# Casts of the count matrix to f16: narrower first range, later ScalarE cast, one cast moved to GpSimd

## The chip, the cores and the metric

The kernel runs on one core of a Trainium2 chip. The metric is the device time of the program in microseconds, the median of several executions. Engines are named as in the profile: PE is TensorE, DVE is VectorE, ACT is ScalarE, POOL is GpSimd, SP is SyncE.

## The reference: what is computed

A graph network of four layers over N = 1024 nodes with D = 512 features and 16384 edges. The graph arrives as two index lists, and three of the layers need it as a matrix. The part that the change touches stands in the first layer:

```
adj = zeros((N, N)); adj[row, col] = 1; adj[col, row] = 1; adj = adj + eye(N)
adj = adj / max(adj.sum(axis=1), 1)
cur = x @ W + b
for i in range(3): cur = adj @ cur; out = out + dw[i + 1] * cur
x = layernorm(x + relu(out))
```

The later layers sum over the edges (with their counts), take means over them, and compute an attention with a softmax over them; each ends in a residual sum and a layernorm.

## The kernel before

**The count matrix.** The edges are worked off in 64 groups of 256 (`NG`). For each, PE multiplies one-hot matrices that DVE and ACT build, and DVE adds the product to a window of the f32 count matrix `c32` (128 partitions x 8 tiles of rows x 1024 columns); this is `add_window`, line 1274, and each addition raises the semaphore `win_free`. The same loop on PE also computes h = xW in f32 (line 774). When the 64th window is added, `c32` is complete. On PE, `attention_columns` (line 810, 32 f32 matmuls of 40 columns for the last layer) stands between the last group and what follows.

**The passage.** From `c32` to the 0/1 matrix `adj` the kernel goes in four steps, tile by tile:

- Casts: `c32` goes to the f16 matrix `cst`, in column ranges given by `CAST_COLS = ((0, 256), (256, 512), (512, 1024))`. For the first two ranges ACT casts row tiles 0 to 2 (`CA` = 3) and DVE row tiles 3 to 7. Of the third range ACT casts tile 7 at once and tiles 5 and 6 later, DVE casts tiles 0 and 1 (line 1343) and later tiles 2 to 4 (line 1360).
- Transposes: `ct_block(t)` on PE (line 871) transposes the t-th block of 128 columns of all 8 row tiles of `cst` into one of three banks of PSUM. It waits for the casts of its range: `chunk_of(t)` is the index of the range in which column block t lies. Block t from 3 on also waits for a free bank.
- Evictions: ACT copies the bank to `cts[:, t, :]` (line 437), and raises `cts_ready`.
- DVE builds row tile t of `adj` from `cst[:, t, :]` and `cts[:, t, :]` (line 1354, a scalar_tensor_tensor with a row sum, 1358 adds the diagonal), and raises `adj_ready`. This needs all 1024 columns of row tile t of `cst`.

PE then multiplies: for each j it waits for `adj_ready` j + 1 and issues 8 matmuls of 512 columns (line 886) that use row tile j of `adj`, with `ct_block(j + 3)` between. After the eighth come the second half of the first step (line 897) and the second and third steps (lines 907, 925).

**The order.** It is written by hand. Each engine has one queue in program order; between engines there are semaphores. On PE stand ct_block(0), (1), then waits for the last pieces of h, (2), (3), then the matmuls. On DVE stand the two casts of line 1313, `h_lower(7)` (line 1279, the low half of the last tile of h), the cast of line 1343, and the loop over t with line 1360 behind t = 1. On ACT stand the three casts, three evictions, the cast of tiles 5 and 6, and five evictions. POOL has done its part of the constants by then: its last instruction ahead of the passage scales a bias (`b0w` times `wsum`, line 394, once DVE has summed the weights), the next (line 383) waits for the first weight's high half, which ACT makes behind the passage. A branch for edges outside their window (`flag(.., 0)`) is not taken.

Of the kernel before, what the change touches and what calls it, by code (L numbers as in the profile page):

```python
# [48 lines left out]
H_FROM = 4  # L49
H_TO = 31  # L50
ZERO_ACT = 6
CAST_COLS = ((0, 256), (256, 512), (512, 1024))
CT_BANKS = (0, 1, 5)
WINDOW_BANKS = (0, 1, 6, 7)

# [40 lines left out]
def build(nc, x, xT, src, dst, W0, b0, dw, W1T, b1, wc, wn, b2, W3, W3T, b3, b3T, aw, ab, out):  # L96
    with ExitStack() as ctx:
# [248 lines left out]
        def _(pool):  # L346
# [31 lines left out]
            pool.affine_select(out=sel[:], in_=sel[:], compare_op=ALU.not_equal, fill=1.0, base=0,  # L378
                               pattern=[[-1, H + 1], [0, P]], channel_multiplier=1).then_inc(S["const_ready"], 1)

            def split_lo(n, name, raw):
                pool.wait_ge(S["w_hi"], n)
                pool.tensor_tensor(ws[:, SLOT[name], 1], raw, ws[:, SLOT[name], 0], ALU.subtract).then_inc(S["w_lo"], 1)  # L383
# [7 lines left out]
            pool.wait_ge(S["wba_a"], 1)  # L391
            pool.tensor_tensor(wba[:], wba[:], wbc[:].unsqueeze(2).broadcast_to([P, KT, H]), ALU.mult).then_inc(S["wba_in"], 1)
            pool.wait_ge(S["wsum_in"], 1)
            pool.tensor_scalar(b0w, b0w, wsum[:], None, ALU.mult).then_inc(S["bias_in"], 1)
            split_lo(1, "W1", stage[:, 0])
            split_lo(2, "wc", stage[:, 1])
# [38 lines left out]
        def _(act):  # L435
# [65 lines left out]
            for c0, c1 in CAST_COLS[0:2]:  # L501
                copy(cst[:, 0:CA, c0:c1], c32[:, 0:CA, c0:c1]).then_inc(S["cst_act"], 1)
            c0, c1 = CAST_COLS[2]
            copy(cst[:, 7:NT, c0:c1], c32[:, 7:NT, c0:c1]).then_inc(S["cst_act"], 1)
            for t in range(NT):
                act.wait_ge(S["ct_done"], t + 1)
                copy(cts[:, t, :], bank16(CT_BANKS[t % 3])).then_inc(S["cts_ready"], 1)
                if t == 2:
                    copy(cst[:, 5:7, c0:c1], c32[:, 5:7, c0:c1]).then_inc(S["cst_act"], 1)
            act.wait_ge(S["const_ready"], 12)  # L510


# [216 lines left out]
        def _(pe):  # L729
# [133 lines left out]
            pe.wait_ge(S["win_free"], NG)  # L863

            def ct_block(t):
                pe.wait_ge(S["cst_act"], (1, 2, 4)[chunk_of(t)])
                pe.wait_ge(S["cst_dve"], (1, 2, 4)[chunk_of(t)])
                if t >= 3:
                    pe.wait_ge(S["cts_ready"], t - 2)
                for j in range(NT):  # L870
                    ins = pe.transpose(bank16(CT_BANKS[t % 3])[:, j * P:(j + 1) * P], cst[:, j, t * P:(t + 1) * P], id16[:])
                ins.then_inc(S["ct_done"], 1)
# [320 lines left out]
        def _(dve):  # L1193
# [123 lines left out]
            with dve.If(flag(dve, 0)):  # L1317

                dve.wait_ge(S["cst_dve"], 2)
                dve.wait_ge(S["cst_act"], 3)  # L1320
                for a in range(NT):
                    ts(iota_n[:, a * P:(a + 1) * P], iota_lo[:], float(a * P), None, ALU.add).then_inc(S["far_iota"], 1)
                dve.wait_ge(S["far_iota"], NT)
                cols_s = nslo[:].rearrange("p g c -> p (g c)")
                cols_f = far.rearrange("p g c -> p (g c)")
                CHUNKS = NC * NG
                with dve.Fori(0, NT) as a:
                    with dve.Fori(0, CHUNKS) as e:
                        n = a * CHUNKS + e
                        dve.wait_ge(S["far_free"], n + 1)  # L1330
                        ts(oh_far, iota_n, cols_f[:, bass.ds(e, 1)], None, ALU.is_equal).then_inc(S["far_hot"], 1)
                        ts(oh_lo, iota_lo[:], cols_s[:, bass.ds(e, 1)], 0.0, ALU.add, ALU.is_equal).then_inc(S["far_hot"], 1)
                    dve.wait_ge(S["far_done"], a + 1)

                    ts(far, far, -float(N), None, ALU.add).then_inc(S["far_added"], 1)
                    tt(c32[:, a, :], c32[:, a, :], ps[:, 0:2, :].rearrange("p a n -> p (a n)"), ALU.add).then_inc(S["far_added"], 1)
                    dve.wait_ge(S["far_added"], a * 2 + 2)
                for j in range(NT):
                    dve.tensor_copy(cst[:, j, :], c32[:, j, :]).then_inc(S["far_cast"], 1)
                dve.wait_ge(S["far_cast"], NT)  # L1340
            dve.wait_ge(S["const_ready"], 12)
            c0, c1 = CAST_COLS[2]
            dve.tensor_copy(cst[:, 0:2, c0:c1], c32[:, 0:2, c0:c1]).then_inc(S["cst_dve"], 1)

            for t in range(NT):
                dve.wait_ge(S["cts_ready"], t + 1)
                if t == 0:
                    dve.wait_ge(S["cst_dve"], 3)
                    dve.wait_ge(S["cst_act"], 2)
                elif t == 2:  # L1350
                    dve.wait_ge(S["cst_dve"], 4)
                elif t == 5:
                    dve.wait_ge(S["cst_act"], 4)
                stt(adj[:, t, :], cst[:, t, :], -1.0, cts[:, t, :], ALU.mult, ALU.is_lt,
                    accum_out=deg[:, t:t + 1]).then_inc(S["adj_sum"], 1)
                dve.wait_ge(S["adj_sum"], t + 1)
                diag = adj[:, t, t * P:(t + 1) * P]
                tt(diag, diag, id16[:], ALU.add).then_inc(S["adj_ready"], 1)
                if t == 1:
                    dve.tensor_copy(cst[:, 2:5, c0:c1], c32[:, 2:5, c0:c1]).then_inc(S["cst_dve"], 1)  # L1360
# [438 lines left out]
```

## Time and profile before

| | us |
|---|---|
| median of 3 runs | 411.85 (411.67 to 411.90) |
| the profiled execution, its own time | 411.46 |
| its span, first to last instruction | 409.5 |
| PE busy | 379.4 (93%) |
| DVE busy | 278.0 (68%) |
| ACT busy | 244.3 (60%) |
| POOL busy | 92.8 (23%) |

Times in the rows are microseconds from the start of the span. A row of the timeline has the start, the duration, the engine, the line, the operation, out<-in with shapes and the count of instructions merged in it; in brackets stands how long the engine was idle before it, and who ended that. Consecutive instructions of DVE or ACT overlap by about 0.09 us in these records. The chain of waits is followed back from the last instruction. PEclk is the granted clock of TensorE, 1.00 for 2.4 GHz and 0.50 for 1.2 GHz.

### The profile page before, as it was taken

The page shows a single profiled execution, that of the slowest core. Times are in us where ns is not written, and L with a number is a line of the kernel's source. Part 1 is how long each engine was busy: PE and PEld are TensorE (multiplying, and loading weights), DVE is VectorE, ACT ScalarE, POOL GpSimd, SP SyncE. Part 2 cuts the span into 40 slices and gives each one's busy share as a digit, 9 for nine tenths or more (in the row PEclk, how much of TensorE's full clock was granted, in tenths as well). Part 3 has the DMA queues.
Part 4 walks back from the last instruction along what each step waited for, and adds up shares of the span by engine and source line. Part 5 has one row for each costly group of instructions (what it writes and reads, how often), then busy time and mean ns, then how long its engine had stood idle before and what let it go on. Part 6 is the DMA issues. An engine that isn't in the chain of part 4 may idle for free.

```text
span 409.5 us, 8229 instructions
## 1 busy us (share of the span) xinstructions
PE 379.4 (93%) x2844; PEld 225.4 (55%) x2844; DVE 278.0 (68%) x603; ACT 244.3 (60%) x406; POOL 92.8 (23%) x85
## 2 busy tenths in 40 slices
PE   1799889999999998999999999999899999999980
PEld 1344438544444443444445454445457889999980
DVE  7768998838995775206633222554699688999974
ACT  9779785475822246202665221247774999999434
POOL 4510000029920167200764000133100000112110
PEclk9999998999999999999999999999999999999996
DMA  5940005006000000000000000000001112210005
GB/s 192 390 151 2 1 0 205 4 0 206 1 0 2 0 0 3 2 0 2 0 0 2 0 0 3 0 0 2 1 2 49 58 64 93 104 55 2 4 3 206
DMA packets 10040, 18.54 MB, mean 45 GB/s; under 512 B 2128, under 2 KB 2320, under 8 KB 10000
## 3 DMA queue, kind: packets, MB, share of 16 engines
q1 hardware_dynamic: 9136, 14.86, 10.4%
q10 hardware_dynamic: 864, 3.15, 2.2%
q8 instruction: 25, 0.41, 0.4%
q14 instruction: 15, 0.12, 0.1%
HBM read 15.87 MB, written 2.13 MB: 44 GB/s over the span
## 4 chain that ended last, share of the span: by engine, by line
PE 72%; DVE 16%; issue 5%; ACT 3%; DVEq 2%; POOL 1%; ACTq 0%; POOLq 0%
PE ps L741 15%; PE ps L1120 9%; PE ps L968 7%; PE ps L1013 7%; PE ps L925 7%; PE ps L907 7%; PE ps L1061 7%; PE ps L774 4%; PE ps L897 3%; DVE c L1274 3%; PE ps L886 3%; PE ps L795 2%; DVE big L1510 1%; DVE adj L1255 1%; DVE cts L1560 1%
## 5 line engine op out<-in xcount | busy, mean ns | idle before, releaser
L741 PE MATMUL ps<-big,xTs 128*128 128x512 f16 x384 | 85.5, 380 | 1.4 <-ACT xTs L437 1.4
L741 PEld LDWEIGHTS ps<-big,xTs 128*128 128x128 f16 (+1 forms) x384 | 36.8, 98 | 44.0 <-issue 2.1
L648 ACT ACTIVATE big<-big,uvt 128x1024 bf16<-128x1024 f32 x55 | 59.0, 1149 | 0.0
L409 POOL TENSOR_TENSOR big<-xcur,big x24 | 27.7, 1155 | 125.2 <-ACT xcur L530 124.8
L529 ACT ACTIVATE big<-xcur,nmr,rstd (+1 forms) x24 | 19.5, 813 | 36.8 <-DVE nmr L1380 36.8
L774 PE MATMUL ps<-big,xTs 128*128 128x512 f32 x64 | 35.7, 655 | 0.0
L437 ACT ACTIVATE xTs<-ps 128x512 f16<-128x512 f32 (+2 forms) x24 | 20.1, 878 | 21.7 <-PE ps L968 19.0
L437 ACT ACTIVATE big<-ps 128x512 f16<-128x512 f32 (+2 forms) x17 | 9.7, 572 | 34.5 <-PE ps L741 24.6
L1274 DVE TENSOR_TENSOR c<-c,ps 128x80 f32 (+31 forms) x64 | 23.3, 364 | 9.7 <-PE ps L795 6.6
L1061 PE MATMUL ps<-big,cst 128*128 128x260 f16 x256 | 29.8, 275 | 0.0
L383 POOL TENSOR_TENSOR big<-xTs,big 128x2048 f16<-128x2048 f32 x4 | 16.2, 4076 | 59.9 <-ACT big L437 59.9
L968 PE MATMUL ps<-cst,big 128*128 128x512 f16 x128 | 27.8, 380 | 1.6 <-DVE xcur L1451 1.6
L795 PE MATMUL ps<-adj,cts 128*128 128x80 f16 (+31 forms) x128 | 21.0, 271 | 8.7 <-DVE c L1274 4.6
L420 POOL TENSOR_TENSOR xcur<-xcur,c 128x512 f32<-128x512 f32 x6 | 7.1, 1185 | 95.5 <-DVE c L1594 95.5
L795 PEld LDWEIGHTS ps<-adj,cts 128*128 128x128 f16 x128 | 11.4, 109 | 31.4 <-issue 16.6
L1013 PE MATMUL ps<-big,cts 128*128 128x512 f16 x128 | 28.0, 379 | 0.0
L925 PE MATMUL ps<-big,adj 128*128 128x512 f16 x128 | 27.9, 380 | 0.0
L907 PE MATMUL ps<-big,adj 128*128 128x512 f16 x128 | 27.8, 380 | 0.0
L1061 PEld LDWEIGHTS ps<-big,cst 128*128 128x128 f16 x256 | 24.3, 96 | 4.8
L460 ACT ACTIVATE cts<-iota_lo,early 128x128 f16<-128x128 f16 x80 | 25.4, 391 | 0.4
L1255 DVE TENSOR_TENSOR adj<-adj,early 128x160 f16<-128x160 f16 (+31 forms) x64 | 22.3, 390 | 0.1
L968 PEld LDWEIGHTS ps<-cst,big 128*128 128x128 f16 x128 | 12.4, 98 | 16.9 <-DVE xcur L1451 2.1
(206 smaller groups left out, 678.3 us busy)
## 6 DMA issues: line engine op xcount, KB each, us to landing
big<-u_rows ACTq DMA_DIRECT2D x6, 512.0 KB, 3.4
xTs<-in_xT SPq DMA_DIRECT2D x2, 1024.0 KB, 9.3
xcur<-in_x SPq DMA_DIRECT2D x1, 2048.0 KB, 17.5
out<-xcur SPq DMA_DIRECT2D x8, 256.0 KB, 2.1
big<-in_W SPq DMA_DIRECT2D x1, 1024.0 KB, 6.0
cts<-in_W3T SPq DMA_DIRECT2D x1, 1024.0 KB, 12.9
xTs<-in_W1T SPq DMA_DIRECT2D x1, 1024.0 KB, 5.4
xTs<-in_wc SPq DMA_DIRECT2D x1, 1024.0 KB, 8.1
```

The source lines that it names most:

```text
L437: return act.activation(o, i, ACT.Copy, scale=scale, **kw)
L648: act.activation(above[:, a % AHEAD, :], uf[:, h % 2], ACT.Relu, scale=BIG, bias=vb[:, j, h:h + 1]).then_inc(S["above_in"], 1)
L741: return mm(bank, lhs(k)[a], rhs(k)[b], start=start and k == 0 and n == 0, stop=stop and k == KT - 1 and n == 2)
L774: ins = mm(bank, xT32[:, k, t * P:(t + 1) * P], w0raw[:, k, :], start=k == 0, stop=k == KT - 1)
L795: ins = mm(ps[:, WINDOW_BANKS[w % 4], 0:n], left, hot_key[:, r, w % 2 * NC * n:(w % 2 + 1) * NC * n].rearrange("p (k c) -> p k c", c=NC)[: ...
L907: ins = mm(ps[:, t, :], adj[:, j, t * P:(t + 1) * P], cur[:, 1, v, j, :], start=n == 0 and v == 0, stop=n == NT - 1 and v == 1)
L925: ins = mm(ps[:, t, :], adj[:, j, bass.ds(t * P, P)], cur[:, 0, v, j, :], start=n == 0 and v == 0, stop=n == NT - 1 and v == 1)
L968: ins = mm(ps[:, half * KT + k, :], cur[:, 1, v, j, k * P:(k + 1) * P], c[:, j, half * HALF:(half + 1) * HALF], start=c is cst and j == 0 ...
L1013: ins = mm(ps[:, t, :], c[:, j, bass.ds(t * P, P)], cur[:, 0, v, j, :], start=c is cts and j == 0 and v == 0, stop=c is parts[-1] and j == ...
L1061: ins = mm(ps[:, DENSE_BANK[i], 0:4 * (DH + 1)], cst[:, j, t * P:(t + 1) * P], yh[:, j, v, 4 * half:4 * half + 4, DH + 1:YW], start=j == 0 ...
L1120: ins = mm(o, cz[h % CZ][:, j, t * P:(t + 1) * P], yh[:, j, v, h, :], start=j == 0 and v == 0, stop=j == NT - 1 and v == 1)
L1274: tt(cells, cells, ps[:, WINDOW_BANKS[w % 4], 0:NT * m].rearrange("p (a w) -> p a w", w=m), ALU.add).then_inc(S["win_free"], 1)
```

## The change

The first range of columns is 128 wide instead of 256, the second 384 instead of 256. ACT no longer casts tile 7 of the third range ahead of its evictions; behind the third eviction it casts tiles 5 to 7 instead of 5 and 6. The cast of tiles 0 and 1 of the third range moves from DVE to POOL, where it stands behind the computation for `wba` and ahead of the scaling of `b0w`; it waits for all 64 windows and raises a new semaphore `cst_pool`. PE waits for `cst_pool` ahead of ct_block(4) to (7), DVE ahead of row tile 0 of `adj`. The other counts of the semaphores follow.

```
-CAST_COLS = ((0, 256), (256, 512), (512, 1024))
+CAST_COLS = ((0, 128), (128, 512), (512, 1024))
 # POOL
             pool.wait_ge(S["wsum_in"], 1)
+            pool.wait_ge(S["win_free"], NG)
+            pool.tensor_copy(cst[:, 0:2, c0:c1], c32[:, 0:2, c0:c1]).then_inc(S["cst_pool"], 1)
             pool.tensor_scalar(b0w, b0w, wsum[:], None, ALU.mult).then_inc(S["bias_in"], 1)
 # ACT
             c0, c1 = CAST_COLS[2]
-            copy(cst[:, 7:NT, c0:c1], c32[:, 7:NT, c0:c1]).then_inc(S["cst_act"], 1)
...
                 if t == 2:
-                    copy(cst[:, 5:7, c0:c1], c32[:, 5:7, c0:c1]).then_inc(S["cst_act"], 1)
+                    copy(cst[:, 5:NT, c0:c1], c32[:, 5:NT, c0:c1]).then_inc(S["cst_act"], 1)
 # PE
-                pe.wait_ge(S["cst_act"], (1, 2, 4)[chunk_of(t)])
-                pe.wait_ge(S["cst_dve"], (1, 2, 4)[chunk_of(t)])
+                pe.wait_ge(S["cst_act"], chunk_of(t) + 1)
+                pe.wait_ge(S["cst_dve"], chunk_of(t) + 1)
+                if chunk_of(t) == 2:
+                    pe.wait_ge(S["cst_pool"], 1)
 # DVE
-            dve.tensor_copy(cst[:, 0:2, c0:c1], c32[:, 0:2, c0:c1]).then_inc(S["cst_dve"], 1)
...
                 if t == 0:
-                    dve.wait_ge(S["cst_dve"], 3)
+                    dve.wait_ge(S["cst_pool"], 1)
+                    dve.wait_ge(S["cst_dve"], 2)
                     dve.wait_ge(S["cst_act"], 2)
                 elif t == 2:
-                    dve.wait_ge(S["cst_dve"], 4)
+                    dve.wait_ge(S["cst_dve"], 3)
                 elif t == 5:
-                    dve.wait_ge(S["cst_act"], 4)
+                    dve.wait_ge(S["cst_act"], 3)
```

DVE's queue from the first cast to the first tile of `adj` (line 1313 casts, 1279 is `h_lower(7)`, 1343 casts tiles 0 and 1, 1354 builds `adj`; `c` is `c32`, the branch not taken is left out), before:

```order
L1313 CAST cst<-c 128x5x256 [waits win_free]
L1313 CAST cst<-c 128x5x256
L1279 TENSOR_TENSOR big<-ps,big 128x512 [waits acc0]
...
L1343 CAST cst<-c 128x2x512 [waits const_ready]
L1354 SCALAR_TENSOR_TENSOR adj,deg<-cst,cts 128x1024 [waits cst_act,cst_dve,cts_ready]
L1358 TENSOR_TENSOR adj<-adj,id 128x128 [waits adj_sum]
```

and now (the lines are shifted by 5 or 6):

```order
L1318 CAST cst<-c 128x5x128 [waits win_free]
L1318 CAST cst<-c 128x5x384
L1284 TENSOR_TENSOR big<-ps,big 128x512 [waits acc0]
...
L1360 SCALAR_TENSOR_TENSOR adj,deg<-cst,cts 128x1024 [waits cst_dve,cst_pool,cst_act,cts_ready,const_ready]
L1364 TENSOR_TENSOR adj<-adj,id 128x128 [waits adj_sum]
```

The third cast has left the queue, and the first tile of `adj` waits for POOL as well. POOL's queue at the same place, before (`wba` and `big` hold small weights and the bias `b0w`):

```order
L390 TENSOR_TENSOR wba<-abT 128x32 [waits small_in]
L392 TENSOR_TENSOR wba<-wba,wbc 128x32 [waits wba_a]
L394 TENSOR_SCALAR big<-big,wsum 128x512 [waits wsum_in]
L383 TENSOR_TENSOR big<-xTs,big 128x2048 [waits w_hi] x2
L387 TENSOR_TENSOR acc<-acc,big 128x512 [waits acc_r,bias_in]
```

and now:

```order
L392 TENSOR_TENSOR wba<-abT 128x32 [waits small_in]
L394 TENSOR_TENSOR wba<-wba,wbc 128x32 [waits wba_a]
L397 CAST cst<-c 128x2x512 [waits win_free,wsum_in]
L398 TENSOR_SCALAR big<-big,wsum 128x512
L385 TENSOR_TENSOR big<-xTs,big 128x2048 [waits w_hi] x2
```

The cast has come in, and the scaling of the bias behind it waits for the windows too. ACT's queue of casts and evictions (`cts<-ps`), before:

```order
L437 ACTIVATE cst<-c 128x3x256 [waits win_free]
L437 ACTIVATE cst<-c 128x3x256
L437 ACTIVATE cst<-c 128x512
L437 ACTIVATE cts<-ps 128x1024 [waits ct_done] x3
L437 ACTIVATE cst<-c 128x2x512
L437 ACTIVATE cts<-ps 128x1024 [waits ct_done] x5
```

and now:

```order
L441 ACTIVATE cst<-c 128x3x128 [waits win_free]
L441 ACTIVATE cst<-c 128x3x384
L441 ACTIVATE cts<-ps 128x1024 [waits ct_done] x3
L441 ACTIVATE cst<-c 128x3x512
L441 ACTIVATE cts<-ps 128x1024 [waits ct_done] x5
```

One cast less stands ahead of the first eviction, and a longer one behind the third.

## Rows read from the trace of the kernel before

**Rows 1.** The page, its part 4: shares of the whole chain by engine.

```profile
PE 72%; DVE 16%; issue 5%; ACT 3%; DVEq 2%; POOL 1%; ACTq 0%; POOLq 0%
```

**Rows 2.** The chain in order of time: start, duration, engine, tile, line.

```profile
64.42 3.50 PE ps L810 x32
...
67.94 1.02 PE ps L871 x8
...
68.99 1.03 ACT cts L437
...
75.73 1.90 PE ps L886 x8
```

**Rows 3.** Timeline of DVE in the passage.

```profile
66.84 1.82 DVE L1313 CAST cst<-c 128x1280 f16<-128x1280 f32 x2
68.58 0.68 DVE L1279 TENSOR_TENSOR big<-ps,big 128x512 f16<-128x512 f32 x1
69.17 0.68 DVE L1343 CAST cst<-c 128x1024 f16<-128x1024 f32 x1
70.05 1.23 DVE L1354 SCALAR_TENSOR_TENSOR adj<-cst,cts 128x1024 f16<-128x1024 f16 x1 [0.20 <-ACT cts L437]
...
71.46 1.22 DVE L1354 SCALAR_TENSOR_TENSOR adj<-cst,cts 128x1024 f16<-128x1024 f16 x1
...
72.86 1.22 DVE L1360 CAST cst<-c 128x1536 f16<-128x1536 f32 x1
```

**Rows 4.** Timeline of ACT: the casts ahead of the evictions, and the late one.

```profile
66.84 2.10 ACT L437 ACTIVATE cst<-c 128x768 f16<-128x768 f32 x3 [1.79 <-DVE c L1274]
...
71.72 1.07 ACT L437 ACTIVATE cst<-c 128x1024 f16<-128x1024 f32 x1
```

**Rows 5.** Timeline of PE, and of its weight loads (PEld).

```profile
67.94 3.57 PE L871 MATMUL ps<-id,cst 128*128 128x128 f16 x32
71.60 3.63 PE L886 MATMUL ps<-big,adj 128*128 128x512 f16 x16
...
75.73 1.41 PEld L886 LDWEIGHTS ps<-big,adj 128*128 128x128 f16 x8 [0.24 <-DVE adj L1358]
```

**Rows 6.** Stretches: length, PE, PEld, DVE, ACT, POOL busy, PEclk, DMA; two matmul rows of PE.

```profile
64.57:67.98 3.41, 3.38 (x31) 3.30 (x31) 3.10 (x6) 1.62 (x3) 0.00 (x0) 1.00 0.72 274
67.98:71.39 3.41, 3.41 (x32) 3.27 (x32) 3.18 (x6) 3.36 (x5) 0.00 (x0) 0.50 0.89 318
...
16.78:20.19 3.41, 3.28 (x12) 1.44 (x11) 2.52 (x11) 1.96 (x6) 0.08 (x1) 1.00 1.05 388
...
20.42 2.02 PE L774 MATMUL ps<-big,xTs 128*128 128x512 f32 x2
...
24.31 0.64 PE L774 MATMUL ps<-big,xTs 128*128 128x512 f32 x1
```

**Rows 7.** Timelines of POOL and DVE where both are at work.

```profile
12.20 0.84 POOL L368 TENSOR_TENSOR cst<-cst 64x256 f32<-64x256 f32 x1
...
12.19 0.27 DVE L1255 TENSOR_TENSOR adj<-adj,early 128x224 f16<-128x224 f16 x1
...
12.37 0.80 DVE L1255 TENSOR_TENSOR adj<-adj,early 128x224 f16<-128x224 f16 x1
...
111.33 4.06 POOL L383 TENSOR_TENSOR big<-xTs,big 128x2048 f16<-128x2048 f32 x1
...
113.16 2.26 DVE L1427 TENSOR_SCALAR cnt<-cnt 128x8 f32<-128x8 f32 x1
```

**Rows 8.** Groups of POOL by line and shape: total, mean ns of one.

```profile
L409 POOL TENSOR_TENSOR big<-xcur,big x24 | 27.7, 1155 | 125.2 <-ACT xcur L530 124.8 <-issue 0.4
...
L383 POOL TENSOR_TENSOR big<-xTs,big 128x2048 f16<-128x2048 f32 x4 | 16.2, 4076 | 59.9 <-ACT big L437 59.9
...
L394 POOL TENSOR_SCALAR big<-big,wsum 128x512 f32<-128x512 f32 x1 | 1.6, 1562 | 0.0
...
L364 POOL CAST cst<-cst 64x256 f32<-64x256 int32 x1 | 0.4, 389 | 0.1
```

More of the change, by code:

```diff
@@ L379, in _ @@
                                pattern=[[-1, H + 1], [0, P]], channel_multiplier=1).then_inc(S["const_ready"], 1)
+            c0, c1 = CAST_COLS[2]
             def split_lo(n, name, raw):
@@ L1319, in _ @@
                 dve.wait_ge(S["cst_dve"], 2)
-                dve.wait_ge(S["cst_act"], 3)
+                dve.wait_ge(S["cst_act"], 2)
+                dve.wait_ge(S["cst_pool"], 1)
                 for a in range(NT):
@@ L1347, in _ @@
                 if t == 0:
-                    dve.wait_ge(S["cst_dve"], 3)
+                    dve.wait_ge(S["cst_pool"], 1)
+                    dve.wait_ge(S["cst_dve"], 2)
                     dve.wait_ge(S["cst_act"], 2)
                 elif t == 2:
-                    dve.wait_ge(S["cst_dve"], 4)
+                    dve.wait_ge(S["cst_dve"], 3)
                 elif t == 5:
-                    dve.wait_ge(S["cst_act"], 4)
+                    dve.wait_ge(S["cst_act"], 3)
                 stt(adj[:, t, :], cst[:, t, :], -1.0, cts[:, t, :], ALU.mult, ALU.is_lt,
```

## The prediction

> **What bounds the kernel now.** The first view is the chain of waits, by engine: PE is 72% of what ended last [rows 1], so a change counts only where it moves PE. The second is the same chain in order of time, around the change [rows 2]. The reader is to see that it never passes through a cast ahead of the first eviction: the f32 products of line 810 hold PE until 67.92, the first eight transposes run from 67.94 to 68.96, ACT evicts from 68.99, DVE starts the first tile of the adjacency at 70.05, and at 75.73 the chain goes back to PE for good. The third view is the timelines of DVE, ACT and PE [rows 3 to 5], which show how close the other engines were. DVE's first two casts take 66.84 to 68.66, so one takes 0.95 and the first is done at 67.79, 0.13 ahead of PE. ACT's three casts end at 68.94, 0.02 ahead of the end of the transposes. DVE is ready at 69.85, 0.20 ahead of the eviction. The weight loads stand idle for 0.24 at 75.73, which cost PE about 0.06; at 71.6 PE waited about 0.1. Those two gaps are all the time that PE loses between 67.94 and the end of this stage.
>
> **The narrower first range.** DVE's casts take 0.68 for 2 tiles of 512 columns, 1.22 for 3, and 0.95 for 5 of 256 [rows 3]. These three fit 0.14 us plus 1.05 ns for each column of the pairs of tiles, an odd tile counting as a pair (1, 2 and 3 pairs). So 5 tiles of 128 take 0.14 + 3 x 128 x 1.05 ns = 0.55, and 5 of 384 take 1.35; together as much as before. The first is done at 67.39 instead of 67.79. ACT's part is ready earlier too. The gain is nil: the transposes wait for PE itself until 67.92. The second block of transposes now hangs on the second cast, which ends at 68.67 if nothing stops it, 0.1 ahead of need (67.94 + 8 x 0.107 = 68.80). This margin is what the change gives away.
>
> **ACT.** Its third cast, 2.10 less two of 0.75, 0.6 us, goes from the front [rows 4]. ACT is then free at 68.4 instead of 68.94, but the first eviction waits for PE until 68.96: gain at most 0.02, taken as nothing. Behind the third eviction it casts 1536 elements a partition instead of 1024: 1.07 + 0.45 = 1.5. The fourth eviction ends near 74.2 instead of 73.7, and DVE wants it at 75.6; PE wants the cast at about 75.0 and has it by 73.3. Both are covered, with 1.4 us to spare.
>
> **DVE.** The cast of line 1343 takes 0.59 of its queue away. It ended 0.20 ahead of the eviction that DVE waits for, so by itself its removal gives nothing; DVE's spare time there becomes 0.8.
>
> **The cast on POOL.** No row shows POOL casting f32 to f16 at this size. The nearest are the cast of 256 elements in 0.39 and the two-input operations, 1.155 for 512 and 4.076 for 2048, that is 0.18 plus 1.90 ns an element [rows 8]. Upper bound: as slow as a two-input one, 2.1. Lower bound: half its rate, for one input, 1.1. The small cast scaled up gives 1.56 with its fixed part counted four times. I take 1.2, nearest to the lower bound, as the small cast less a fixed part of 0.15 comes to 0.94 ns an element. If POOL ran undisturbed from 66.9 it would be done by 68.1, two microseconds ahead of need.
>
> It isn't undisturbed. Two places show DVE and POOL shutting each other out [rows 7]. At 113.16 DVE works on 8 elements and takes 2.26 us: it ends at 115.42, when POOL's operation of 111.33 to 115.39 does. At 12.20 POOL starts an operation while DVE runs the first of two equal ones; DVE's first takes 0.27, its second, which has nothing to wait for, 0.80, and it ends 0.13 after POOL's, at 13.17. So POOL goes in between two operations that stand back to back on DVE, and the second waits until POOL is through. The two casts of DVE are such a pair, and POOL's cast is released by the same semaphore as the first.
>
> The Trainium skill, "SBUF — State Buffer", section "Who interferes with whom", says that DVE in a mode that uses both ports and GpSimd hold one pair of ports by turns, for the whole instruction, and that the order of issue decides who waits. By that rule this change costs something whichever starts first. Both rows above agree with it (0.80 and 2.26 us).
>
> **The sum.** DVE's first cast ends at 67.39; POOL has the port until 68.6; DVE's second cast, 1.3 beyond that, ends at 69.9 instead of 68.66. The second block of transposes starts at 70.0 instead of 68.8. PE at 1.2 GHz needs 0.86 for it, and 0.2 passes until ACT sees the end: eviction 71.05 to 72.05. DVE's second tile then starts at 72.06 instead of 71.46: 0.6 late. The first tile: `h_lower` ends at 70.5, but POOL's queue has a second operation right behind the cast, the scaling of the bias, moved here from 27.84. Its bounds are 1.56 (its row [rows 8]) and 0.7 (half of the cast's 1.2 and a little). It follows DVE's second cast, from 69.9 to 70.6, and DVE's first tile, with two operands in SBUF, starts at 70.6 instead of 70.05: 0.55 late, which the 0.6 of the second tile swallows; by the upper bound it is 1.4 late. From there the chain on DVE is the old one, and the third column's matmuls go from 75.73 to about 76.3. PE itself is no bound there: its remaining transposes end near 72.0 and 16 matmuls at 0.216 and 8 transposes bring it to 75.9. After that PE is continuous as before, so the shift stays. Sum +0.6, with the scaling's length somewhat towards its upper bound +0.7. Against the profiled execution 411.46 + 0.7 = 412.2; it lay 0.39 under the median, and on the median the forecast is 411.85 + 0.7 = **412.6**. The bounds of POOL's two durations make it +0.4 to +1.4.
>
> **Rivals.**
>
> *A, the clock stays down: slower.* From 67.98 to 71.39 PE ran at 1.2 GHz, and it rose to 2.4 behind a stretch in which PE was busy throughout, 3.41 of 3.41 [rows 6]. My sum puts a gap of 1.0 us into it. Early in the span PE was busy for 3.28 of 3.41 from 16.78 to 20.19, and the two f32 matmuls behind took 1.01 each, half rate; at 24.31 one took 0.64 with its fill (the clock column reads 1.00 there only because its record begins later). Against it: what those matmuls fed in was sparser than a string of transposes. If the clock stays down for as long again, to 74.8, the rest of the transposes ends at 72.6, the 16 matmuls (3.45 us at full rate, 1.1 of it done by 74.8) at 77.15, the next transposes at 77.6: 1.9 late. Time 411.85 + 1.9 = 413.8. It decides once PE's gap in that stretch is long enough.
>
> *B, nothing happens.* POOL's cast and scaling, 1.2 and up to 1.56, run from 66.9 to 69.7 beside DVE's casts, which would need the port to be free for both. For it: near 28.6 DVE's operations kept their pace beside the scaling. Then all is in place at 70.05, and the time is 411.85. It can be no gain: the two gaps of PE, 0.15 together, are out of reach, as the first eviction waits for PE.
>
> *C, POOL gets the port first.* Then DVE's first cast runs from 68.05 to 68.6, the scaling goes in between (to 69.3 at least), the second cast ends at 70.65, and `h_lower` at 71.2. The first block of transposes starts 0.8 late, the second at 70.75, the second tile of DVE at 72.75: +1.3, 413.2. Against it: DVE's and ACT's casts started 0.03 after the last window, while a signal to another engine's idle queue takes POOL about as long or longer.
>
> **How the numbers follow.** A measurement of this kernel tells 0.2% (0.82 us) from no change. My case has 0.36, and two thirds of it lie within 0.82; A has 0.30, B 0.18, C 0.10. 0.06 are left for a gain that no row shows, such as a clock that does not fall. Within 0.2%: 0.24 + 0.18, rounded to 0.41. Slower: 0.13 + 0.30 + 0.10 = 0.53. Faster: 0.06. The range goes from B with the spread of the runs, 411.7, to A with the bounds of POOL's durations, 414.1; the likeliest case's own range is 412.2 to 413.3.
>
> **What would show it.** In the new profile: DVE's second cast takes 2.5 us or ends after 69.5 (a duration near 1.35 makes the sum wrong, and B right); POOL's cast lasts 1.1 to 2.1 of its own time; the first block of transposes starts at 67.94 (later: C); PE has a gap of about 1.2 before the second block; the granted clock rises near 71.4 (at 74.8: A); the third column's matmuls start near 76.3. The forecast falls if POOL doesn't enter between the two casts, or if its cast is far from 1.2.

## The result and the profile after

| | before | changed |
|---|---|---|
| median of 22 runs each | 411.44 us (410.80 to 411.95) | 412.07 us (411.09 to 413.17) |
| ratio to before | | 1.0015, 95% interval 1.0008 to 1.0022 |
| the profiled execution, its own time | 411.46 | 412.29 |
| its span | 409.5 | 410.4 |

The change costs 0.6 us, 0.15%. That is under the 0.2% of the forecast's "no change", but the interval lies clear of 1. The medians hide how it comes about: the runs of before lie within 1.2 us, those of the changed kernel within 2.1.

In the chain in order of time a piece has come in that was not there before: DVE's second cast. Start, duration, what (against [rows 2]):

```profile
66.77 0.33 DVE cst L1318
...
67.32 1.99 DVE cst L1318
...
69.45 0.61 PE ps L876 x8
...
71.89 4.37 PE ps L891 x16
...
76.71 1.73 PE ps L891 x8
```

The first piece is the first cast, the second is the second one with its wait. PE's products of line 813 (810 before) no longer stand in this part of the chain. The timelines of POOL and DVE in the changed kernel show why (against [rows 3]; the same operation has a line number 2 to 6 higher):

```profile
66.87 1.22 POOL L397 CAST cst<-c 128x1024 f16<-128x1024 f32 x1 [38.46 <-DVE c L1279]
68.08 2.26 POOL L398 TENSOR_SCALAR big<-big,wsum 128x512 f32<-128x512 f32 x1
...
66.77 0.56 DVE L1318 CAST cst<-c 128x640 f16<-128x640 f32 x1
...
66.77 2.53 DVE L1318 CAST cst<-c 128x640 f16<-128x640 f32 x2
69.22 0.67 DVE L1284 TENSOR_TENSOR big<-ps,big 128x512 f16<-128x512 f32 x1
69.81 1.21 DVE L1360 SCALAR_TENSOR_TENSOR adj<-cst,cts 128x1024 f16<-128x1024 f16 x1
...
71.21 1.22 DVE L1360 SCALAR_TENSOR_TENSOR adj<-cst,cts 128x1024 f16<-128x1024 f16 x1
```

DVE's first cast takes 0.56 and ends at 67.33. POOL's cast, waiting since 66.87, ends at 68.09. DVE's second cast ends at 69.30, 1.21 later, where the pair of before took 1.82 in all. The profile of line 1318 has its two durations, the shortest and the longest:

```profile
L1318 DVE CAST cst<-c x2: 559/1308/2058, 66.8 to 67.2; 128x640 f16<-128x640 f32 x1, 128x1920 f16<-128x1920 f32 x1
```

PE shows the rest (against [rows 5]); the stretches below it have length, PE, PEld, DVE, ACT, POOL busy, PEclk and DMA (against [rows 6]):

```profile
67.68 0.62 PE L876 MATMUL ps<-id,cst 128*128 128x128 f16 x8
69.45 2.44 PE L876 MATMUL ps<-id,cst 128*128 128x128 f16 x24 [1.15 <-DVE cst L1318]
71.69 4.58 PE L891 MATMUL ps<-big,adj 128*128 128x512 f16 x16
...
66.79:70.21 3.42, 2.22 (x28) 1.93 (x28) 3.42 (x4) 2.69 (x4) 3.34 (x2) 1.00 0.98 356
70.21:73.63 3.42, 3.42 (x21) 2.21 (x20) 3.35 (x7) 3.42 (x4) 0.13 (x1) 0.50 0.40 153
73.63:77.00 3.37, 3.37 (x23) 1.74 (x22) 3.03 (x7) 1.01 (x2) 0.00 (x0) 1.00 0.03 5
```

There is a gap of 1.15 us ahead of the second block of transposes. And the clock is at 1.2 GHz in another stretch than before: from 70.21 to 73.63 instead of 67.97 to 71.38. In the kernel before, the low stretch lay over the 32 transposes. Here it lies over the last of them and the first matmuls: 16 matmuls take 4.58 instead of 3.63, and the third column's start 9.78 after DVE's first cast instead of 8.89. The stage from the last window to line 897 or 902 is 0.88 longer (21.51 instead of 20.63), which is the whole difference of the two spans. The stage as one stretch, before and changed:

```profile
66.81:87.44 20.63, 20.46 (x138) 12.39 (x138) 17.02 (x37) 12.89 (x14) 0.00 (x0) 0.92 0.22 80
66.74:88.25 21.51, 20.31 (x138) 11.75 (x138) 17.12 (x36) 12.98 (x13) 3.47 (x2) 0.92 0.23 83
```

PE is busy for 20.31 of 21.51, where it was busy for 20.46 of 20.63. So between these two executions the low stretch, 3.4 us long in both, takes no more from PE; what has grown is PE's idle time, 1.20 instead of 0.17.

The executions of the changed kernel, sorted by the mean granted clock of the whole span, fall into three groups, which the experiments below ask about:

| mean clock | changed, 22 runs | their times |
|---|---|---|
| 0.988 to 0.992 | 9 | 411.09 to 411.58 |
| 0.984 to 0.985 | 6 | 411.63 to 412.43 |
| 0.981 | 7 | 412.67 to 413.17 |

### The profile page after: what moved, and what is told of

Its sections match the earlier page's. It is cut to its first block, busy times and chain, and to the rows that moved or that the text cites. A ratio compares the mean times of both kernels' runs of the same rounds, so it can differ in the third digit from the quotient of the medians.

```text
span 410.4 us, 8234 instructions
## 1 busy us (share of the span) xinstructions
PE 379.0 (92%) x2844; PEld 224.4 (55%) x2844; DVE 278.1 (68%) x602; ACT 244.7 (60%) x405; POOL 94.8 (23%) x86
## 4 chain that ended last, share of the span: by engine, by line
PE 72%; DVE 16%; issue 6%; ACT 3%; DVEq 2%; POOL 1%; ACTq 0%; POOLq 0%
PE ps L744 15%; PE ps L1125 9%; PE ps L973 7%; PE ps L1018 7%; PE ps L930 7%; PE ps L912 7%; PE ps L1066 7%; PE ps L891 4%; DVE c L1279 4%; PE ps L902 3%; PE ps L777 3%; DVE big L1516 1%; DVE adj L1260 1%; PE ps L798 1%; DVE cts L1566 1%
## 5 line engine op out<-in xcount | busy, mean ns | idle before, releaser
L441 ACT ACTIVATE big<-ps,invdeg 128x512 f16<-128x512 f32 x16 | 10.3, 687 | 19.1 <-PE ps L912 14.9
```

The lines of the kernel that those rows point to most:

```text
L441: return act.activation(o, i, ACT.Copy, scale=scale, **kw)
```

## Experiments

The theory after the result: POOL's cast holds the port between DVE's two casts; this makes a gap on PE; the gap costs nothing where the clock is up; and it costs through a granted clock that stays low, or is low at another place, in a part of the executions. The rivals: the ranges cost by themselves; the delay of DVE's chain costs, as the prediction had it; POOL's second operation costs. Each ratio is against runs of the kernel before on the same chip, between those of the others.

### Undoing the cast on POOL

```
-            pool.wait_ge(S["win_free"], NG)
-            pool.tensor_copy(cst[:, 0:2, c0:c1], c32[:, 0:2, c0:c1]).then_inc(S["cst_pool"], 1)
...
             dve.wait_ge(S["const_ready"], 12)
+            dve.tensor_copy(cst[:, 0:2, c0:c1], c32[:, 0:2, c0:c1]).then_inc(S["cst_pool"], 1)
```

> The changed kernel with the cast of tiles 0 and 1 back on DVE, at its old place behind h_lower; ranges and ACT's late cast stay changed. Theory (the cast on POOL enters between DVE's two casts and holds the second up): the second cast lasts about 1.35 us and ends near 68.65, the second block of transposes follows the first without a gap, and the time is that of the kernel before (ratio 1.000, within 0.001). Rival (the narrower first range costs by itself, since the second block now hangs on the later cast): PE keeps a gap ahead of the second block and the time stays about 0.6 us over before.

Measured: 411.43, ratio 1.0001 (0.9992 to 1.0010). DVE and PE in its trace:

```profile
66.17 1.82 DVE L1316 CAST cst<-c 128x640 f16<-128x640 f32 x2
...
69.27 1.23 DVE L1358 SCALAR_TENSOR_TENSOR adj<-cst,cts 128x1024 f16<-128x1024 f16 x1
...
67.07 0.62 PE L874 MATMUL ps<-id,cst 128*128 128x128 f16 x8
68.13 1.71 PE L874 MATMUL ps<-id,cst 128*128 128x128 f16 x24 [0.44 <-DVE cst L1316]
70.82 3.63 PE L889 MATMUL ps<-big,adj 128*128 128x512 f16 x16 [0.98 <-DVE adj L1362]
```

The two casts take 1.82 again, so the cost is the cast on POOL. The gap ahead of the second block is 0.44 and not none, since in this execution the clock was at 2.4 GHz throughout the passage and the first block took 0.62 instead of 1.02 [rows 2]. The last row is the one that the prediction lacked: with the clock up PE waits 0.98 for DVE's first tile ahead of the matmuls. So much of a delay can be taken up there while the clock is up.

### The ranges alone

```
-CAST_COLS = ((0, 256), (256, 512), (512, 1024))
+CAST_COLS = ((0, 128), (128, 512), (512, 1024))
```

> The kernel before with the new column ranges alone (128, 384, 512). Theory: the second cast of DVE ends near 68.65, just ahead of the second block of transposes (68.8 at 1.2 GHz); ratio 1.000, and in executions in which the first block runs at 2.4 GHz up to 0.2 us of gap. Rival (the ranges cost by themselves): ratio 1.001 or more.

Measured: 411.45, ratio 1.0004 (0.9995 to 1.0013). The gap was 0.44, more than the 0.2 that I had allowed, with the clock up and the first block done in 0.62. Neither gain nor loss can be told.

### The cast on POOL alone

```
+            pool.wait_ge(S["win_free"], NG)
+            pool.tensor_copy(cst[:, 0:2, c0:c1], c32[:, 0:2, c0:c1]).then_inc(S["cst_pool"], 1)
             pool.tensor_scalar(b0w, b0w, wsum[:], None, ALU.mult).then_inc(S["bias_in"], 1)
...
-            dve.tensor_copy(cst[:, 0:2, c0:c1], c32[:, 0:2, c0:c1]).then_inc(S["cst_dve"], 1)
```

> The kernel before with one part of the change: the cast of tiles 0 and 1 on POOL, at its new place, ranges and ACT as before. Theory: POOL still enters between DVE's casts, for the 0.76 us between the end of DVE's first cast (67.33) and the end of POOL's (68.09) in the changed kernel; the second cast ends near 69.4 instead of 68.66, but with a first range of 256 columns only the third block of transposes hangs on it, which started near 69.65, so PE sees no gap and the time is that of before (ratio 1.000, within 0.001). Rival (POOL's share of the port costs wherever the ranges lie): ratio about 1.0015.

Measured: 411.49, ratio 1.0010 (1.0001 to 1.0019), at the upper edge of the first expectation; the interval does not tell it from the 1.0015 of the rival. PE in its trace:

```profile
67.30 1.05 PE L877 MATMUL ps<-id,cst 128*128 128x128 f16 x16
69.39 1.05 PE L877 MATMUL ps<-id,cst 128*128 128x128 f16 x16 [1.04 <-DVE cst L1319]
70.84 3.63 PE L892 MATMUL ps<-big,adj 128*128 128x512 f16 x16 [0.39 <-DVE adj L1365]
```

"PE sees no gap" was wrong. I had reckoned with transposes at 1.2 GHz, as in the trace of before; at 2.4 GHz two blocks are done by 68.35, and the gap of 1.04 has only moved behind them. In this execution it costs nothing: ahead of the matmuls PE waits 0.39 for DVE, where it waited 0.98 in the first experiment, and they start 4.65 after DVE's first cast in both.

### POOL's cast behind DVE's second

```
+            pool.tensor_scalar(b0w, b0w, wsum[:], None, ALU.mult).then_inc(S["bias_in"], 1)
             pool.wait_ge(S["win_free"], NG)
+            pool.wait_ge(S["cst_dve"], 2)
             pool.tensor_copy(cst[:, 0:2, c0:c1], c32[:, 0:2, c0:c1]).then_inc(S["cst_pool"], 1)
-            pool.tensor_scalar(b0w, b0w, wsum[:], None, ALU.mult).then_inc(S["bias_in"], 1)
```

> The changed kernel with POOL's two operations at other times: the scaling of the bias ahead of the cast, where it was before, and the cast waiting for DVE's second cast. Theory: DVE's second cast lasts 1.35 us, POOL's cast runs from 68.7 to 69.5 and is done ahead of the first tile of the adjacency (about 69.9), so the time is that of before (ratio 1.000, within 0.001). Rival (the cast on POOL costs by its later signal, or by holding DVE's first tile of the adjacency): that tile starts after 70.1, and the ratio is 1.001 or more.

Measured: 411.28, ratio 0.9997 (0.9988 to 1.0006). The scaling stands ahead of the cast again, as before the change. POOL and DVE:

```profile
68.57 1.04 POOL L399 CAST cst<-c 128x1024 f16<-128x1024 f32 x1 [38.92 <-DVE cst L1319]
...
66.61 1.82 DVE L1319 CAST cst<-c 128x640 f16<-128x640 f32 x2
...
69.79 1.22 DVE L1361 SCALAR_TENSOR_TENSOR adj<-cst,cts 128x1024 f16<-128x1024 f16 x1 [0.77 <-POOL cst L399]
```

Between DVE's casts and its first tile of the adjacency POOL's cast takes 1.04. DVE waits 0.77 for it, and its first tile starts 3.18 after its first cast did, later than the 3.04 of the changed kernel; yet this version is the faster one. So a later first tile of that size costs nothing by itself. That takes out one of the two ways over DVE's chain; the other, a late second tile, is taken out by the changed kernel's own profile (71.21, 4.44 after the first cast, where it was 4.62).

### The scaling ahead of the cast

```
+            pool.tensor_scalar(b0w, b0w, wsum[:], None, ALU.mult).then_inc(S["bias_in"], 1)
             pool.wait_ge(S["win_free"], NG)
             pool.tensor_copy(cst[:, 0:2, c0:c1], c32[:, 0:2, c0:c1]).then_inc(S["cst_pool"], 1)
-            pool.tensor_scalar(b0w, b0w, wsum[:], None, ALU.mult).then_inc(S["bias_in"], 1)
```

> The changed kernel with the scaling of the bias ahead of the cast on POOL, where it was before the change. In the changed kernel it took 2.26 us (68.08 to 70.34) beside DVE's second cast and first tile of the adjacency, yet that tile took its usual 1.21. Theory: the place of the scaling costs nothing, ratio 1.001 to 1.002 as for the changed kernel. Rival (the scaling holds up DVE's first tile, as the prediction had it): ratio below that of the changed kernel by 0.001 and the first tile starts earlier than 3.04 us after the last window.

Measured: 412.64, ratio 1.0030 (1.0018 to 1.0041), 6 runs, all with a mean clock of 0.985 or less. It is no faster than the changed kernel, so the scaling's place isn't the cost. That it came out above the 1.001 to 1.002 of the expectation I can't explain; the two intervals overlap. All six runs fell into the two lower groups, where 13 of the changed kernel's first 22 did, and its first tile starts 3.05 after DVE's first cast, not 3.04. Its profiled execution runs as rival A of the prediction has it: the third column's matmuls start 1.67 later than before, measured from DVE's first cast, where A had 1.9. Stretches:

```profile
64.70:68.11 3.41, 3.41 (x37) 3.41 (x36) 3.10 (x6) 1.61 (x3) 1.28 (x1) 1.00 0.89 289
68.11:71.53 3.42, 2.33 (x24) 2.12 (x22) 3.18 (x5) 2.29 (x4) 0.01 (x1) 0.50 0.89 317
71.53:74.95 3.42, 3.42 (x14) 1.49 (x12) 3.23 (x5) 3.22 (x4) 0.00 (x0) 0.50 0.02 8
74.95:78.36 3.41, 3.41 (x23) 1.82 (x22) 2.19 (x6) 0.81 (x1) 0.00 (x0) 1.00 0.02 5
```

The clock fell about where it fell in the trace of before, at the end of the f32 products of 40 columns. There PE was busy for 3.41 of 3.41 behind the fall and the clock rose at 71.38 [rows 6]. Here PE was busy for 2.33 of 3.42, and the clock stayed down until 74.95.

### The same gap without POOL, and a longer one

Both are made from the kernel of the first experiment.

```
             ct_block(0)
+            pe.wait_ge(S["h_lo"], NT)
             ct_block(1)
```

> The kernel of e1 (cast back on DVE, ratio 1.0001) with one more wait on PE: the second block of transposes waits for the last h_lower of DVE, which ends about 2.35 us after the last window, so that PE has a gap of about 1 us and POOL does nothing. DVE's queue is untouched. Theory (the gap on PE is what costs, through the clock): times spread to 412.5 and more with mean clocks of 0.984 and below, ratio 1.001 to 1.002. Rival (it is POOL's or the port's own doing): ratio 1.000.

Measured: 411.22, ratio 1.0002 (0.9993 to 1.0010): the median does not move, against my expectation; by the ratio alone the rival's 1.000 would have it. The clocks do change: 5 of 11 runs have a mean clock of 0.985 or less. Four of them still lie at 411.17 to 411.96; the fifth, at 412.69, is the profiled one. The gap was 0.84, where the changed kernel's is 1.15, and in that execution (span 410.9) the clock was down from 68.1 to 74.9 as above, with POOL at rest:

```profile
68.11:71.53 3.42, 2.58 (x27) 2.31 (x24) 3.29 (x7) 2.48 (x4) 0.00 (x0) 0.50 0.88 313
71.53:74.95 3.42, 3.42 (x13) 1.49 (x12) 3.28 (x5) 3.04 (x3) 0.00 (x0) 0.50 0.04 16
```

```
             ct_block(0)
+            pe.wait_ge(S["cst_pool"], 1)
             ct_block(1)
```

> The kernel of e8 (no cast on POOL, a wait on PE ahead of the second block of transposes) with a longer gap: it waits for DVE's third cast, about 2.95 us after the last window, so the gap is about 1.5 us. The second eviction ends at up to 5.0 instead of 4.5 us after the last window, which is worth up to 0.4 us on DVE's chain. Theory (the longer the gap, the more executions run the matmuls at 1.2 GHz): ratio 1.002 to 1.004, most executions at mean clocks of 0.985 and below. Rival (only the 0.4 on DVE's chain counts): 1.001 or less, one group.

Measured: 412.63, ratio 1.0027 (1.0016 to 1.0038), 7 runs, none under 411.69. The gap was 1.55. This one doesn't tell the two causes apart as I meant it to: only 3 of 7 runs have a mean clock of 0.985 or less, and the profiled execution, at 2.4 GHz throughout the passage, still has a span of 409.9. Two runs with a mean clock of 0.988 are nearly as slow as the three with a low one (412.53 and 412.63, against 412.65 to 412.67). In the profiled execution the second tile of DVE starts 4.78 after the first cast, 0.27 later than in the first experiment, and PE waits 0.34 for DVE ahead of the third column. So a gap of 1.55 costs something over DVE's chain even with the clock up; the 1.04 of the cast on POOL alone didn't.

### Filling the gap

```
             ct_block(0)
+            for _ in range(2):
+                for j in range(NT):
+                    pe.transpose(bank16(6)[:, j * P:(j + 1) * P], cst[:, j, 0:P], id16[:])
             ct_block(1)
```

> The changed kernel with 16 more transposes of the first column block, into a bank that nobody reads, between the first and the second block of transposes. They take about 0.86 us of the 1.15 us gap at 2.4 GHz. Theory (what costs is the granted clock: the gap in PE's work makes some executions run a stretch of matmuls at 1.2 GHz): the executions near 413 us with a mean clock of 0.981 become rare, and the ratio is 1.0000 to 1.0008. Rival (what costs is the time by which POOL delays the second block, at whatever clock): 1.0015 or more, as the filling takes nothing from that delay.

Measured: 411.64, ratio 1.0006 (0.9995 to 1.0016), 12 runs. None has a mean clock below 0.986. Nothing of POOL's or DVE's delay is taken away: DVE's casts take 2.53 as in the changed kernel. Stretches of its profiled execution:

```profile
67.88:71.29 3.41, 3.41 (x36) 3.41 (x34) 3.38 (x5) 1.59 (x3) 2.51 (x2) 0.50 0.93 337
71.29:74.70 3.41, 3.41 (x28) 1.84 (x26) 2.42 (x5) 3.41 (x4) 0.00 (x0) 1.00 0.11 43
```

The clock fell at nearly the same place as in the experiment with the scaling (67.88 and 68.11), but now PE is busy until 71.29, and it rises there. Six of the runs, this one among them, are at 0.986 and 412.05 to 412.44: at 1.2 GHz the filling takes 1.91 us, over twice the 0.86 that I had reckoned at 2.4 GHz, and holds the real transposes up. The other six are at 410.31 to 411.23. So work for its own sake is not a cure. But with POOL's delay intact no run is in the lowest group, where the scaling ahead of the cast had three of its six runs on the same chip, and the two intervals (0.9995 to 1.0016, 1.0018 to 1.0041) don't touch. It is PE's gap that keeps the clock down for a second stretch. Against the changed kernel's own interval (1.0008 to 1.0022) the filled one is not clear.

### The changed kernel again, and half the cast

> The changed kernel once more, beside the next three on one chip. Theory (the cost comes with the granted clock): ratio 1.001 to 1.003, and times in groups: near 411.3 with mean clocks of 0.988 and more, near 412.2 at 0.984 to 0.985, near 413 at 0.981. Rival (a fixed delay of the chain): one group 0.6 us above before.

Measured: 412.07, ratio 1.0012 (1.0003 to 1.0021), the same groups: 4 of 12 runs at 0.988 and more (411.27 to 411.46), 6 at 0.984 to 0.985 (411.34 to 412.39), 2 at 0.981 (412.57, 413.01).

```
-            pool.tensor_copy(cst[:, 0:2, c0:c1], c32[:, 0:2, c0:c1]).then_inc(S["cst_pool"], 1)
+            pool.tensor_copy(cst[:, 0:1, c0:c1], c32[:, 0:1, c0:c1]).then_inc(S["cst_pool"], 1)
...
             dve.wait_ge(S["const_ready"], 12)
+            dve.tensor_copy(cst[:, 1:2, c0:c1], c32[:, 1:2, c0:c1]).then_inc(S["cst_one"], 1)
```

> The changed kernel with one size changed: POOL casts tile 0 alone (512 columns), DVE casts tile 1 behind h_lower (0.41 us). POOL's hold between DVE's casts falls from 0.76 to about 0.4 us, so PE's gap ahead of the second block falls from 1.15 to about 0.8. Theory: ratio between that of the ranges alone (1.0004) and that of the changed kernel: 1.0002 to 1.001. Rival (any operation of POOL in that place costs the same): as the changed kernel of this batch.

Measured: 411.74, ratio 1.0005 (0.9996 to 1.0014), 1 of 11 runs below 0.987. The gap was 0.73. POOL and DVE:

```profile
66.27 0.79 POOL L397 CAST cst<-c 128x512 f16<-128x512 f32 x1 [37.98 <-DVE c L1280]
67.05 2.26 POOL L398 TENSOR_SCALAR big<-big,wsum 128x512 f32<-128x512 f32 x1
...
66.16 2.11 DVE L1319 CAST cst<-c 128x640 f16<-128x640 f32 x2
...
68.78 0.80 DVE L1350 CAST cst<-c 128x512 f16<-128x512 f32 x1
```

The ratio is where the theory had it, but its interval holds both 1 and the changed kernel's 1.0012. DVE's casts take 2.11: 0.29 of waiting instead of 0.71. The cast of one tile on DVE takes 0.80, where the same takes 0.41 in the next experiment, without POOL: here the scaling on POOL does hold DVE up, as it did not hold up the first tile of the adjacency in the changed kernel.

### Two versions without POOL

ACT takes 2 row tiles instead of 3 in the first ranges, DVE 6 instead of 5; of the third range ACT casts tile 0 ahead of its evictions and tiles 5 to 7 behind the third, and DVE tile 1 alone. The second version has 8 transposes that nobody reads in the gap. From the kernel with the ranges alone:

```
-CA = 3
+CA = 2
...
-            copy(cst[:, 7:NT, c0:c1], c32[:, 7:NT, c0:c1]).then_inc(S["cst_act"], 1)
+            copy(cst[:, 0:1, c0:c1], c32[:, 0:1, c0:c1]).then_inc(S["cst_act"], 1)
...
-                    copy(cst[:, 5:7, c0:c1], c32[:, 5:7, c0:c1]).then_inc(S["cst_act"], 1)
+                    copy(cst[:, 5:NT, c0:c1], c32[:, 5:NT, c0:c1]).then_inc(S["cst_act"], 1)
...
-            dve.tensor_copy(cst[:, 0:2, c0:c1], c32[:, 0:2, c0:c1]).then_inc(S["cst_dve"], 1)
+            dve.tensor_copy(cst[:, 1:2, c0:c1], c32[:, 1:2, c0:c1]).then_inc(S["cst_dve"], 1)
```

> A version without POOL: ranges of 128, 384, 512 columns; ACT casts 2 row tiles instead of 3 in the first two ranges and then tile 0 of the third ahead of its evictions; DVE casts 6 instead of 5 (an odd tile costs as much as a pair) and only tile 1 of the third range; ACT's late cast takes tiles 5 to 7. By the rows DVE's queue is free 0.3 us earlier and the first eviction is unchanged, so the first tile of the adjacency starts about 2.75 us after the last window instead of 3.1. Theory (with PE at 2.4 GHz the chain on DVE is the bound): 0.3 us faster where the clock is up in the passage, less where it is down: ratio 0.9993 to 1.0000. Rival (PE is the bound throughout): 1.000.

> The rebalanced kernel e9 (no POOL, ratio 0.9997) with 8 transposes that nobody reads between the first and the second block, in a gap of 0.45 us at 2.4 GHz. Theory (a fuller stretch keeps the clock up more often): ratio 0.998 to 1.000. Rival (where the clock is down anyway the filling delays PE by up to 0.4 us): 1.000 to 1.001.

Measured: 411.13, ratio 0.9997 (0.9988 to 1.0005), and 411.32, ratio 0.9998 (0.9989 to 1.0006). DVE of the first:

```profile
66.66 1.83 DVE L1313 CAST cst<-c 128x768 f16<-128x768 f32 x2
68.41 0.68 DVE L1279 TENSOR_TENSOR big<-ps,big 128x512 f16<-128x512 f32 x1
69.01 0.41 DVE L1343 CAST cst<-c 128x512 f16<-128x512 f32 x1
69.51 1.22 DVE L1354 SCALAR_TENSOR_TENSOR adj<-cst,cts 128x1024 f16<-128x1024 f16 x1
```

Six tiles take as long as five (1.83 and 1.82), and the first tile starts 2.85 after the first cast, where it was 3.10 in the first experiment and 3.21 before. In its profile, with the clock up, the passage from DVE's first cast to line 897 takes 20.24, 0.25 less than in the first experiment, as expected; the medians don't tell it from no change. For the second version neither the theory's gain nor the rival's loss can be told. No version beats the kernel before by more than its measurement.

### All runs by their clock

| kernel | gap ahead of the waiting block, us | runs | mean clock 0.983 or less | 0.984 to 0.986 | 0.987 or more | ratio |
|---|---|---|---|---|---|---|
| before | none at 1.2 GHz | 94 | 0 | 2 | 92 | 1 |
| POOL behind (e5) | 0.44 | 11 | 0 | 0 | 11 | 0.9997 |
| ranges alone (e4) | 0.44 | 11 | 0 | 0 | 11 | 1.0004 |
| cast back (e1) | 0.44 | 11 | 0 | 3 | 8 | 1.0001 |
| rebalanced (e9) | 0.45 | 11 | 0 | 0 | 11 | 0.9997 |
| half the cast (e12) | 0.73 | 11 | 0 | 1 | 10 | 1.0005 |
| gap alone (e8) | 0.84 | 11 | 1 | 4 | 6 | 1.0002 |
| POOL alone (e3) | 1.04 | 11 | 0 | 2 | 9 | 1.0010 |
| scaling first (e2) | 1.09 | 6 | 3 | 3 | 0 | 1.0030 |
| changed (both series) | 1.15 | 34 | 9 | 12 | 13 | 1.0015, 1.0012 |
| gap longer (e10) | 1.55 | 7 | 0 | 3 | 4 | 1.0027 |
| changed, filled (e7) | filled | 12 | 0 | 6 | 6 | 1.0006 |
| rebalanced, filled (e11) | filled | 12 | 0 | 2 | 10 | 0.9998 |

The runs with a low mean clock don't simply grow with the gap: they are 5 of 11 at 0.84, 2 of 11 at 1.04, 21 of 34 at 1.15 and 3 of 7 at 1.55. The mean clock holds the end of the span too, where PE has nothing to do and the clock is at 1.2 GHz for 6.4 to 9.1 us, so it is a rough sieve. The profile of before, with one low stretch in the passage, stands at 0.987, that of half the cast at 0.988, that of the changed kernel at 0.985. A profile is needed to say where the stretches lie. In the profiles, from the start of DVE's first cast to line 897 or its like:

| profiled execution | low stretches in the passage | PE idle, us | length, us |
|---|---|---|---|
| cast back (e1) | none | 1.53 | 20.49 |
| POOL alone (e3) | none | 1.52 | 20.50 |
| gap longer (e10) | none | 1.95 | 20.77 |
| before | one | 0.17 | 20.60 |
| half the cast (e12) | one | 1.05 | 21.09 |
| changed, each of two | one | 1.20 | 21.48 |
| changed, filled (e7) | one | 0.38 | 21.47 |
| gap alone (e8) | two | 0.84 | 22.14 |
| scaling first (e2) | two | 1.09 | 22.26 |

With the clock up, PE is idle for 1.5 us of the passage, with the cast on POOL or without it. One low stretch uses this time up: the kernel before, with one, is only 0.11 longer than the first experiment's without. In the changed kernel the gap can't be made up any more then, and it costs most of its length: 0.88 against before. A second low stretch costs some 0.8 more. Filling the gap (its transposes count as work here) takes away the second stretch, but not the loss with one (21.47).

## Why the prediction was right, and where its steps were not

The forecast was 412.6, +0.17%, and the range 411.7 to 414.1; measured are 412.07 and +0.15%. The number came out by a sum of which one half holds: that its +0.7 lies beside the measured +0.6 is luck, since the median is one of a mixture that the sum doesn't have.

**The first casts.** Forecast 0.55 for 5 tiles of 128 columns, measured 0.56; the second 1.35, measured 1.35 without a wait (1.82 for both in the first experiment, less 0.56, plus the overlap of 0.09 in the records). Counting an odd tile as a pair held for 3 and 5 tiles, but a single tile of 512 columns took 0.41 and not the 0.68 of two. That the narrower range gains nothing held (1.0004).

**POOL between DVE's casts.** It held, in each profile with POOL's cast at that place (2.53, 2.53, 2.40 and 2.11 us for DVE's two casts against 1.82). The term was mis-sized: I took 1.2 for POOL with bounds of 1.1 and 2.1, and it keeps DVE for 0.71 to 0.76. Alone the cast takes 1.04, under my lower bound, and by an estimate from the two (1.04 less 0.76) some 0.3 of it ran before the port was free. The Trainium skill, "SBUF — State Buffer", section "Who interferes with whom", has the exclusive lock that goes by the order of issue. The trace agrees for the casts: POOL's cast stands from 66.87 and ends 0.76 after DVE's first. Of POOL's second operation it does not show such a lock against DVE's first tile, as the next paragraph says.

**The second operation on POOL.** Wrong: forecast was a first tile of the adjacency at 70.6, held by the scaling; it started at 69.81 and took its usual 1.21, though the scaling's record runs to 70.34, and moving the scaling away gained nothing. Only the cast of a tile on DVE was held by it (0.80 instead of 0.41).

**The chain on DVE, and "PE itself is no bound there".** This is the step that failed. I let the second eviction end at 72.05, because the first two blocks of transposes ran at 1.2 GHz in the trace of before. In the changed kernel's profile the first ran at 2.4 GHz and the evictions came in time: DVE's second tile starts 4.44 after its first cast, 0.18 earlier than before (4.62), not 0.6 later. The whole +0.6 of my sum is not there. What bounds the third column is PE: I had its 16 matmuls and 8 transposes done by 75.9, but the matmuls took 4.58, as the low stretch lay over them and behind the gap, and the third column started at 76.55. I had read PE's waits, 0.15 in all, from one execution in which a low clock happened to fill them. With the clock up PE waits 0.98 there in the first experiment, and a gap of 1.15 should fit in almost whole: no execution of the changed kernel with the clock up was profiled, but 13 of its 34 runs are at 411.1 to 411.6, where before is. With one low stretch that waiting is gone, and the gap becomes PE's own loss, 1.20 of idle time instead of 0.17.

**Rival A, the clock stays down.** Its mechanism makes a part of the cost. In my book it had 0.30 and a time of 413.8, 1.9 over before; 9 of 34 runs are in its group, at 412.57 to 413.17, 1.1 to 1.7 over the median of before. Twelve more are at 411.34 to 412.43: in the two that were profiled the clock is down for one stretch, and the gap costs most of its length (0.88 against before). The median falls into that group. So what I called one of two outcomes is a share of the changed kernel's runs (none of 94 of before are in the lowest group), and the right sum would have weighed three cases: no low stretch, one, two. That the gap can keep the clock down is shown by the filling (nobody in the lowest group, with POOL's delay intact) and by the profile of the gap without POOL; that gap alone didn't move the median, so how often it happens at a given gap is not settled, nor what makes the clock fall in the first place.

**Rival B** has lost: POOL's and DVE's casts did not run beside each other. **Rival C** has lost too: DVE's first cast took 0.56, and POOL entered behind it.

**The signs named beforehand.** DVE's second cast was to last 2.5 us or end after 69.5: it ended at 69.30 and lasted 2.06. The gap was to be 1.2: 1.15. The clock was to rise near 71.4, or at 74.8 for A: it rose at 73.63, because it had fallen at another time. The third column's matmuls were to start near 76.3: 76.55, held by PE and not by DVE. Two slips in the prediction's figures change nothing: by its own terms "within 0.2%" is 0.42 and "slower" 0.52, not 0.41 and 0.53, and A has the gap at 1.0 where the sum has 1.2.

## What to carry to other kernels

A cast that is moved from DVE to POOL leaves DVE's queue, but if both use the shared port it doesn't leave DVE's time: here 0.59 us of DVE's own became 0.71 of waiting, at an earlier and worse place. Before a stage is said to be tight on PE, look at what the clock was in the profiled execution; slack that a low clock has eaten is there in the other executions, and where it is eaten a new gap costs most of its length. And count a gap ahead of dense work at more than its length, if it comes while the clock is down: it may keep it down.

## What the runs showed of the hardware

- The low stretch of TensorE's clock begins at another time in each execution: at 67.97 (before) and 68.11 (scaling first, gap alone) behind the f32 products of 40 columns, at 70.21 in the changed kernel, and not at all in the first experiment's profile. In the latter PE had run the same products. In the changed kernel it fell after PE had been busy for 2.22 of 3.42 us; in the first experiment PE was busy for 2.28 of 3.43 from 67.07 on, and it stayed up. What makes it fall is open.
- DVE's cast of f32 to f16 in SBUF costs as much for 5 row tiles as for 6: with 128 and 384 columns 1.82 and 1.83 together. A single tile of 512 columns takes 0.41, two take 0.68.
- POOL's cast of 1024 elements a partition from f32 to f16 takes 1.04 where DVE casts nothing. Its record includes the wait for DVE: 1.22 in the changed kernel, 1.48 where DVE's first cast was 0.95 long.
- The scaling of 512 elements on POOL has 2.26 us in its record beside DVE's casts, and 1.56 [rows 8] where it stood before.
